# Softmax over the batch: maxima taken in steps of 2048 elements from one PSUM buffer, and the sum in one step of 4096

## The reference, cut to what matters

```
Q = (x @ Wq.T + bq).reshape(B, S, H, dk)      # B 32, S 256, H 16, dk 8; K and V alike
scores = jnp.einsum('bqhd,bkhd->hbqk', Q, K)
attn = jax.nn.softmax(scores, axis=1)         # axis 1 is the batch
heads = jnp.einsum('hbqk,bkhd->bqhd', attn, V).reshape(B, S, dm)
return heads @ Wo.T + bo
```

## Time and profile before

| | us |
|---|---|
| median of 3 runs | 1695.55 (1689.3 to 1696.78) |
| the profiled execution | 1693.03 |
| its span, first to last instruction | 1691.3 |
| attention stage, about | 103 to 818 |

### The profile page before, as it was taken

One profiled execution on the slowest core, in us unless ns is written; L12 is line 12 of the kernel. 1 busy time (PEld: TensorE's weight loads), 2 busy tenths in 40 slices (PEclk: granted clock), 3 DMA queues, 4 the chain that ended last, 5 costly groups with the idle time before them and its releaser, 6 DMA issues. The chain is left out here.

```text
span 1691.3 us, 42035 instructions
## 1 busy us (share of the span) xinstructions
PE 1392.7 (82%) x14758; PEld 1078.4 (64%) x14759; DVE 1242.4 (73%) x2603; ACT 885.9 (52%) x1437; POOL 1029.3 (61%) x746
## 2 busy tenths in 40 slices
PE   7858999999999999998189968888888099999940
PEld 5635666666666666665179966667667099999940
DVE  5559999999999999998356646999998523333346
ACT  7818888888888888887034422222222044444420
POOL 6624888888888888889534432656556544444420
PEclk9859999999999999999589988999999599999975
DMA  6863333333333333310533321222221122222248
GB/s 221 270 197 95 77 83 82 83 82 84 82 82 83 84 80 86 81 50 18 138 123 99 94 60 59 90 94 82 89 93 54 50 63 68 66 65 65 65 138 289
DMA packets 117937, 163.58 MB, mean 97 GB/s; under 512 B 18592, under 2 KB 85408, under 8 KB 113184
## 3 DMA queue, kind: packets, MB, share of 16 engines
q1 hardware_dynamic: 92960, 123.42, 26.3%
q0 software_dynamic: 13600, 28.45, 5.1%
q10 hardware_dynamic: 11232, 9.73, 1.8%
HBM read 99.52 MB, written 62.01 MB: 96 GB/s over the span
## 5 line engine op out<-in xcount | busy, mean ns | idle before, releaser
L921 ACT ACTIVATE Ex<-pB 128x512 f32<-128x512 f32 x512 | 514.3, 1081 | 84.5 <-PE pB L731 80.2
L962 POOL TENSOR_TENSOR V<-Ex,R 128x4096 f32<-128x4096 f32 x64 | 474.2, 7409 | 98.8 <-DVE R L841 98.7
L819 DVE TENSOR_REDUCE mg<-pA 128x128 f32<-128x1024 f32 x256 | 297.5, 1203 | 3.7 <-PE pA L714 3.4
L835 DVE TENSOR_REDUCE Z<-Ex 128x64 f32<-128x2048 f32 x128 | 290.7, 2273 | 4.6 <-ACT Ex L921 4.5
L731 PEld LDWEIGHTS pB<-qk 72*128 72x128 bf16 x2048 | 157.7, 97 | 122.5 <-issue 1.1
L726 PE MATMUL pB<-mh,identb 128*128 128x512 bf16 x512 | 196.6, 384 | 36.0 <-ACT Ex L921 35.4
L1113 POOL DMA_INDIRECT y_d<-x1yb,x1xb x136 | 130.2, 957 | 151.4 <-DVE x1yb L1228 146.8
L731 PE MATMUL pB<-qk 72*128 72x128 bf16 x2048 | 198.9, 219 | 0.0
L726 PE MATMUL pB<-ml,identb 128*128 128x512 bf16 x512 | 194.0, 379 | 0.0
L741 PE MATMUL pO<-V,Vh 128*8 128x128 f32 x4096 | 161.0, 278 | 12.9 <-POOL V L962 12.8
L714 PE MATMUL pA<-qk 72*128 72x128 bf16 x2048 | 162.5, 224 | 8.8 <-DVE mg L819 4.9
(11 more groups left out here) (232 smaller groups left out, 2368.1 us busy)
## 6 DMA issues: line engine op xcount, KB each, us to landing
qk<-qs_d SPq DMA_DIRECT2D x96, 192.0 KB
qk<-ks_d SPq DMA_DIRECT2D x96, 192.0 KB
x1xb<-xs_d SPq DMA_DIRECT2D x136, 64.5 KB
f_ye<-y_d SPq DMA_DIRECT2D x16, 512.0 KB, 5.9
qs_d<-parts SPq DMA_DIRECT2D x16, 384.0 KB, 2.9
ks_d<-parts SPq DMA_DIRECT2D x16, 384.0 KB, 3.2
x0xb<-xs_d SPq DMA_DIRECT2D x72, 64.5 KB
xn_d<-xn SPq DMA_DIRECT2D x16, 258.0 KB, 3.3
```

Source lines behind the costliest of these rows:

```text
L819: dve.tensor_reduce(mg[:, :, g], pA[:, g % 2, :, :].rearrange("p b q -> p q b"), AX.X, ALU.max).then_inc(b_red, 1)
L835: dve.tensor_reduce(Z[:, q], Ex[:, j, q, :], AX.X, ALU.add).then_inc(b_sum, 1)
L921: act.activation(Ex[:, j, :, BG * g:BG * (g + 1)].rearrange("p q b -> p b q"), pB[:, g % 2, :, :], ACT.Exp).then_inc(b_exp, 1)
L962: pool.tensor_tensor(En[:, j % 2, :, :].rearrange("p b q -> p q b"), Ex[:, j, :, :], R[:, j % 2, :].unsqueeze(2).broadcast_to([P, P, B]), ...
```

## The change

- GM doubles to 16: a unit has NM = 2 groups of 16 sequences (2048 columns), and `pA` is one buffer in place of two halves, of the same size in all. A group of s1 now waits for the maximum of the group just before it.
- `group_max` takes the maximum of 2048 elements, twice a unit in place of four times 1024. `mg` is P x NM: it now has two columns in place of four, so that `unit_max` reads 256 elements in place of 512.
- The two half sums become one `unit_sum` of 4096 elements.
- DVE's turn becomes: first group maximum, sum, reciprocal, second group maximum, unit maximum.
- PE's turn has s1 ahead of s2 groups 0 and 4, and no longer ahead of 2 and 6.

```diff
-            GM = 2 * BG
+            GM = 4 * BG
...
-            pA = pb("pA", [P, 2, GM, P], ph)
+            pA = pb("pA", [P, GM, P], ph)
...
-                    if not isinstance(n, int) or n >= 2:
-                        pe.wait_ge(b_red, n - 1)
+                    if not isinstance(n, int) or n >= 1:
+                        pe.wait_ge(b_red, n)
...
-                        ins = nc.tensor.matmul(pA[:, g % 2, c, :],
+                        ins = nc.tensor.matmul(pA[:, c, :],
...
-                            s1(g // 2)
+                            if g % (NBG // NM) == 0:
+                                s1(g // (NBG // NM))
...
-                    dve.tensor_reduce(mg[:, :, g], pA[:, g % 2, :, :].rearrange("p b q -> p q b"),
+                    dve.tensor_reduce(mg[:, :, g], pA[:].rearrange("p b q -> p q b"),
...
-                def half_sum(v, j, i):
+                def unit_sum(v, j):
...
-                    q = slice(i * P // 2, (i + 1) * P // 2)
-                    dve.tensor_reduce(Z[:, q], Ex[:, j, q, :], AX.X, ALU.add).then_inc(b_sum, 1)
+                    dve.tensor_reduce(Z[:], Ex[:, j, :, :], AX.X, ALU.add).then_inc(b_sum, 1)
...
                         if summed:
-                            half_sum(v, vj, 0)
+                            unit_sum(v, vj)
+                            inverse(v, vj)
                         if more:
                             group_max(u + 2, 1)
-                            group_max(u + 2, 2)
-                            group_max(u + 2, 3)
                             unit_max(u + 2, (j + 2) % 4)
-                        if summed:
-                            half_sum(v, vj, 1)
-                            inverse(v, vj)
```

More of the change, by code:

```diff
@@ L827, in unit_max @@
                     dve.tensor_reduce(nm[:, j, :], mg[:], AX.X, ALU.max, negate=True).then_inc(b_nm, 1)
-                def half_sum(v, j, i):
+                def unit_sum(v, j):
                     dve.wait_ge(b_exp, NBG * v + NBG)
-                    if i == 0 and (not isinstance(v, int) or v >= 1):
+                    if v >= 1:
                         dve.wait_ge(b_r, v)
-                    q = slice(i * P // 2, (i + 1) * P // 2)
-                    dve.tensor_reduce(Z[:, q], Ex[:, j, q, :], AX.X, ALU.add).then_inc(b_sum, 1)
+                    dve.tensor_reduce(Z[:], Ex[:, j, :, :], AX.X, ALU.add).then_inc(b_sum, 1)
                 def inverse(v, j):
-                    dve.wait_ge(b_sum, 2 * v + 2)
+                    dve.wait_ge(b_sum, v + 1)
                     if not isinstance(v, int) or v >= 2:
@@ L892, in _ @@
                 last = 4 * H - 1
-                half_sum(last, 3, 0)
-                half_sum(last, 3, 1)
+                unit_sum(last, 3)
                 inverse(last, 3)
```

## The result

| | before | changed |
|---|---|---|
| median, us | 1692.57 (4 runs, 1689.3 to 1696.78) | 1723.93 (4 runs, 1721.56 to 1724.91) |
| the profiled execution | 1693.03 | 1724.91 |
| its span | 1691.3 | 1723.2 |

The ratio is 1.0197, with a 95% interval of 1.0173 to 1.0222: the changed kernel is slower by 31 us. The forecast was 1720, in a range of 1707 to 1738.

The account below looks back on a forecast made before the run. DVE bounds the kernel before; after the change, a ring of waits between DVE and PE. Turns +19.5, tail +0.2 and start +7 make +26.7 us on 1693.03, so 1720, with 1707 to 1738 for 8 in 10.

Parts of the forecast that it names:

- the ring: Closed chain of waits between DVE and PE, first maximum to next: 10.89 us a turn, 0.33 more than before.
- DVE's own cost: DVE's steps after the change, at 1.04 ns an element: 10.29 us a turn if DVE were all that counted.
- The handover: From the second maximum's end, through PE's s1, to the next first maximum: 1.15 us in each turn.
- PE and ACT: Whether they outlast the ring: PE free at 9.45, second maximum ended at 9.74, so early by 0.3 us.
- The start of the stage: First maxima in a ring with 16 matmuls at the low rate: +7 us, between 5.5 and 9.
- The tail: POOL's work alone, behind the last turn, moves later: +0.2 us.
- rival 1: The handover is hidden and DVE alone counts: turn 10.29 us, time 1684 us; chance 0.05.
- rival 2: Fixed costs of two maxima and a sum fall away, 0.44 us, not 0.19: 1705 with the ring; chance 0.08.
- rival 3: PE and ACT are the longer ring: with 0.4 us more on each turn, 1744 us; chance 0.13.
- rival 4: The clock falls as PE pauses once in each turn: 1768 us; chance 0.04.

Follow-up runs that it names:

- e1: The changed kernel with its one sum split into two half sums again, one between the two group maxima; 1680.93 us, ratio to the kernel before 0.9921.
- e5: The changed kernel with 8 matmuls more in the second s1 group of each unit; 1725.36 us in one run.
- e3: The changed kernel with PE's wait for the loads of q and k taken one s2 pair earlier; 1720.88 us in one run.

## Why the prediction was right

**The bound.** The turn of the ring through DVE as the price of the stage held: 59 turns carry 23.0 of the 31 us.

**DVE's own cost.** The steps forecast as 2.15, 4.44, 0.87 and 2.31 came as 2.20, 4.45, 0.87 and 2.26. The unit maximum's record is 0.42, as forecast. The 0.05 more stands with the maximum that had to wait. The other's record, which the ring contains, was put at 2.28 and is 2.23, so in the ring the two errors cancel, and that is luck. Without any wait, the maxima of 2048 took 2.14 and 2.32 us (early turns of e1) where the four of 1024 took 4.59: 0.13 us saved by two operations fewer, and 0.05 by one sum fewer (4.45 for 2.19 + 2.31). The Trainium skill, Perfetto Trace Analysis, Optimizing Scalar/DVE Operations, would have it at 0.31 together, an estimate from its figures; the runs show 0.18 and speak for the steps of the earlier trace rows.

**The handover.** It was forecast as 1.15 us from the maximum's end to the next first maximum. It is 401.37 - 400.20 = 1.17 in the short turns and 412.35 - 411.12 = 1.23 in the long ones. The mis-sized part is the second semaphore: the wait was taken as 0.04 everywhere, from a group that waits for one, and half of the first groups wait for two. That is 0.06 to 0.08 in half of the turns. With the 0.02 of the short turns it makes 0.39 a turn in place of 0.33, so 23.0 us in place of 19.5.

**PE and ACT.** "Early by 0.3 us in the worst turn" was right. The changed kernel's PE, in the turn that starts at 401.37:

```profile
409.48 0.39 PE L726 MATMUL pB<-mh,identb 128*128 128x512 bf16 x1
...
410.24 0.62 PE L741 MATMUL pO<-V,Vh 128*8 128x128 f32 x16
```

The last s2 group starts 8.11 us into the turn (forecast 8.15), PE is free at 9.49 (9.45), and the second maximum ends at 9.75 (9.74): early by 0.26. With 0.45 us more in e5's second group the turn stayed as it was, but little of PE's wait was left. PE with ACT as the longer ring was weighed for this order alone; in e1's order it sets the turn, at 10.30.

**The start of the stage.** Forecast: maxima 4.2 to 4.3 us apart and s2 later by 6.9. The rows that answer to the earlier trace rows:

```profile
110.82 2.28 DVE L820 TENSOR_REDUCE mg<-pA 128x128 f32<-128x2048 f32 x1
115.09 2.29 DVE L820 TENSOR_REDUCE mg<-pA 128x128 f32<-128x2048 f32 x1 [1.98 <-PE pA L714]
...
119.43 2.29 DVE L820 TENSOR_REDUCE mg<-pA 128x128 f32<-128x2048 f32 x1 [1.59 <-PE pA L714]
123.70 2.29 DVE L820 TENSOR_REDUCE mg<-pA 128x128 f32<-128x2048 f32 x1 [1.98 <-PE pA L714]
...
127.97 2.29 DVE L820 TENSOR_REDUCE mg<-pA 128x128 f32<-128x2048 f32 x1 [1.53 <-PE pA L714]
```

and those to the earlier trace rows:

```profile
127.73 0.63 PE L726 MATMUL pB<-mh,identb 128*128 128x512 bf16 x1
...
147.65 1.87 PE L714 MATMUL pA<-qk 72*128 72x128 bf16 x16 [2.05 <-DVE mg L820]
```

s2 starts 127.73 - 110.82 = 16.91 us after the first maximum, before 9.99: +6.92. The whole start came to +7.8, not +7. The rest fits one more group at the low rate: PE stood 2.05 us before the first group of unit 4, and its 16 matmuls then took 1.87 us where later ones take 1.07. The granted clock, at 1.00 just before, read 0.50, the lower of its two levels, from about 147.5 to 154.4 us; in the kernel before it read 1.00 from 130 us on. From reciprocal to reciprocal that turn lasted 11.80 us, 0.9 more than a short one.

**The tail** came as +0.3, forecast +0.2.

**The rivals.** The handover was never hidden in the changed order (rival 1). The fixed costs did not fall away: 0.18 us, not 0.44 (rival 2). PE with ACT did not set the turn (rival 3), but did in e1. The clock stayed at 1.00 in the steady part but for its first 5 us, with PE pausing in each turn (rival 4). What the working did not see is how near the better kernel lay: it argued that no saving on DVE can turn the ring round, which is true of the ring as ordered, and one moved half sum undid the ring.

## What to carry to other kernels

The buffer that two engines handed to and fro cost here, once in each round, the filling and both signals, and cost nothing where the waiting engine had other work at just that place: price the gap at each handover against the work that the order puts there. Half a sum and the reciprocal in the gap were worth more here (10.95 - 10.30 = 0.65 us a turn) than the operation saved by merging (0.05). Before a step is moved, look up which waits it was covering.

## What the runs showed of the hardware that was not expected

- A second semaphore wait ahead of a matmul that is waited for cost 0.08 us, though its condition had been met (e3: turns of 10.99 became 10.91).
- A reduction of 4096 fp32 elements from SBUF took 4.41 us, one of 2048 from PSUM 2.23 to 2.29, one of 1024 from PSUM 1.22. From start to start, where the next one waits for nothing, that was 1.04 to 1.07 ns an element (2.14 and 2.19 for 2048, 1.08 for 1024), and each operation saved gave only 0.05 to 0.07 us.
- A reduction of 512 elements was followed by the next after 0.60 us where that one did not wait for it, and after 0.79 where it did.
- After a pause of 2.05 us PE's 16 matmuls took 1.87 us, as at the start of the stage, and not 1.07, with the granted clock at 0.50 (its lower level) until 154.4 us; in e5 it fell likewise, at about 152 us, behind a pause of 1.60. With pauses of 0.4 to 0.6 us in every turn it stayed at 1.00.
